# Moving one batch's normalisation ahead of another batch's scatter, from GpSimd to VectorE, and the next batch's projections to other units

## The chip, the core and the metric

The kernel runs on one core of one Trainium2 chip. The metric is device time in microseconds (us) of that core. Engines are named as in the profile: PE is TensorE, DVE is VectorE, ACT is ScalarE, POOL is GpSimd, SP is the engine that issues most DMAs. Each engine runs its own instruction stream in order and waits for the others on semaphores.

## The reference

The input is x of 8 batches x 512 tokens x 256 features, float32. Three sub-layers follow each other, each with a residual:

```
x = x + 0.5 * ffn(layernorm(x))
x = x + attn(layernorm(x))
x = x + 0.5 * ffn(layernorm(x))
```

`ffn` is a routed mixture of experts: a sigmoid picks one of 4 groups, the group's 2 experts (256 -> 512 -> 256, silu(gate) * up) are weighted by normalised sigmoid scores:

```
macro_scores = sigmoid(xf @ macro_w)            # 4 groups; the best one is taken
micro_scores = sigmoid(einsum('td,gde->tge', xf, micro_w))
out = einsum('te,tef,efd->td', w, silu(gate) * up, down_w)
```

`attn` has 16 heads of 16 features and works on windows of 128 tokens at a stride of 64, so 7 windows per batch:

```
scores = einsum('bhnqd,bhnkd->bhnqk', qw, kw) * scale + pos_bias
ow = einsum('bhnqk,bhnkd->bhnqd', softmax(scores), vw)
merged = zeros.at[:, :, flat].add(ow)           # overlapping windows are added,
merged = merged / counts                        # then divided by their count
return merged_as_rows @ Wo + bo
```

## The kernel before

The program has three stages. In the first, all 4096 tokens are normalised and routed; each token's row (its features, mean, reciprocal deviation, token number and two expert weights) is scattered to DRAM so that the tokens of a group lie together, and the first ffn goes over 35 tiles of 128 rows. The second stage is attention, and inside it, batch by batch, the routing for the second ffn. The third stage is the second ffn.

The change lies in the attention stage. A batch is 28 **units** (7 windows x 4 quarters of the heads); `batch(b, par, first_, last)` is written once for each engine. `two_by_two` (line 312) calls it for batch 0, then in a hardware loop of three turns for batches 1 and 2, 3 and 4, 5 and 6, then for batch 7. In a unit PE computes scores two units ahead (L1028, two units at a time), transposes four probability tiles (L846, `turn`) and multiplies with the values (L1055, `values`); DVE adds the bias and finds the row maximum two units ahead (L1491, `biased`), and copies the transposed probabilities out of PSUM (L1501, `copy_pt`); ACT takes the exponential (L806). After each window PE spreads the reciprocal sums (L1066, `factors`), DVE weighs the result (L1515, `weigh`) and POOL adds it into `ctxt` (L572, `accumulate`).

Between these, each unit has room for a piece of **side work**, and tables of unit numbers say which: `PE_SIDE`, `ACT_SIDE`, `DVE_SIDE` for a middle batch, `..._FIRST` for batch 0 and `..._LAST` for batch 7 (lines 281 to 300). DVE's table counts two units ahead and ACT's one behind: an entry at 16 in DVE's table runs in DVE's unit 14, one at 16 in ACT's in ACT's unit 17. While batch b runs, the side work is:

- for batch b+1: the norm (`bn_stats`, L1547, on DVE; the small arithmetic, L598 to L607, and the normalising itself, L612, on POOL), its transposes (`turn_prep`), their copies out of PSUM (`copy_prep`, L702, on ACT), and the projections to k and q (`k0a` to `q1b`, L983, copied out by ACT, L776 and L782) and to v (`v0` to `v3`, L998, copied out by DVE, L1481). Next batch's scores, which PE starts in unit 26, need all of k and q.
- for batch b-1: the output projection (`o0` to `o3`, L1011), the residual add on DVE (L1521), then the router: norm (`r_stat`, again with L612 on POOL), `turn_route`, logits (`l0` to `l3`), the exponential (L706), the best group (`best_groups`, L1256 to L1259, on DVE), `choose` (the first of equal groups, running counts, expert weights) and `find_place` on POOL, with PE's `rank` between them, and at last `scatter`: four indirect DMAs issued by POOL (L506), which write the batch's rows to their places.

POOL's order at a change of batch is what the change works on. At the end of batch b it runs `find_place` and `scatter` for batch b-1, and only then, at the head of batch b+1, `memset` of `ctxt` (L663) and `norm` for batch b+2, whose xa tiles PE's `turn_prep` waits for. In the middle batches `turn_prep` stands in unit 5 of PE. All DMAs of a batch but the scatter are issued by SP in order: the shifts of the values, the reload of `stage` with batch b-1's residual rows (L445), which must wait until the previous scatter has landed, and the load of `xb` for the norm (L428).

## Time and profile before

| | us |
|---|---|
| median of 3 runs | 1509.48 (1508.91 to 1517.62) |
| the profiled execution | 1505.25, span 1503.5 |
| attention stage, DVE's first copy of batch 0 to its first of batch 7 | 528.5 to 1054.9 |
| PE busy | 1254.1, 83% of the span |
| DVE busy | 842.9, 56% |
| ACT busy | 667.3, 44% |
| POOL busy | 372.3, 25% |

The shares are over the whole span; the attention stage is read by batch from the row of times in which each batch's 28 copies (L1501) start. The clock column of a window view is the mean TensorE clock granted in it: 1.00 is 2.4 GHz, 0.50 is 1.2 GHz. Idle time before an instruction is given in square brackets with what ended it.

### The profile page before, as it was taken

The page shows a single profiled execution, that of the slowest core. Times are in us where ns is not written, and L with a number is a line of the kernel's source. Part 1 is how long each engine was busy: PE and PEld are TensorE (multiplying, and loading weights), DVE is VectorE, ACT ScalarE, POOL GpSimd, SP SyncE. Part 2 cuts the span into 40 slices and gives each one's busy share as a digit, 9 for nine tenths or more (in the row PEclk, how much of TensorE's full clock was granted, in tenths as well). Part 3 has the DMA queues.
Part 4 walks back from the last instruction along what each step waited for, and adds up shares of the span by engine and source line. Part 5 has one row for each costly group of instructions (what it writes and reads, how often), then busy time and mean ns, then how long its engine had stood idle before and what let it go on. Part 6 is the DMA issues. An engine that isn't in the chain of part 4 may idle for free. (4 is left out here: it accounts for less than half of the span.)

```text
span 1503.5 us, 33781 instructions
## 1 busy us (share of the span) xinstructions
PE 1254.1 (83%) x8771; PEld 813.0 (54%) x8772; DVE 842.9 (56%) x3419; ACT 667.3 (44%) x2395; POOL 372.3 (25%) x624
## 2 busy tenths in 40 slices
PE   4422599999999499989899888989963899999997
PEld 4422366666666255555556555555542466666665
DVE  5689544444444277776667666757853344444443
ACT  1105322222323278776767676858750222223222
POOL 3322111111111322353434343443343011111111
PEclk9999999999999799998999899989975899999999
DMA  9600452000000310110010102020106121000000
GB/s 302 224 22 25 155 182 58 23 14 14 14 14 15 98 36 9 43 51 15 25 44 23 43 10 57 2 65 2 51 26 252 47 63 53 14 14 14 14 14 18
DMA packets 51758, 81.36 MB, mean 54 GB/s; under 512 B 7424, under 2 KB 35328, under 8 KB 51648
## 3 DMA queue, kind: packets, MB, share of 16 engines
q1 hardware_dynamic: 44832, 61.29, 12.8%
q0 software_dynamic: 6816, 18.81, 3.5%
q8 instruction: 45, 0.74, 0.2%
q14 instruction: 65, 0.53, 0.1%
HBM read 45.81 MB, written 27.97 MB: 49 GB/s over the span
## 5 line engine op out<-in xcount | busy, mean ns | idle before, releaser
L895 PE MATMUL bank<-w_all,xt 128*128 x1680 | 389.5, 382 | 11.7 <-DVE xt L1343 3.5
L806 ACT ACTIVATE w_all<-w_all 128x128 f32<-128x128 f32 x896 | 346.7, 392 | 95.1 <-DVE w_all L1491 93.4
L895 PEld LDWEIGHTS bank<-w_all,xt 128*128 128x128 f16 x1680 | 164.9, 98 | 195.7 <-issue 35.6
L1491 DVE CUSTOM_DVE_ANT_0 w_all<-bank,w_all 128x128 f32<-128x128 f32 x896 | 197.6, 285 | 77.6 <-ACT w_all L806 40.8
L1331 DVE SCALAR_TENSOR_TENSOR hb<-bank,ew,sl 128x512 f32<-128x512 f32 x140 | 105.1, 751 | 206.4 <-ACT sl L717 206.4
L913 PE MATMUL bank<-w_all,ht 128*128 x1680 | 206.2, 273 | 1.2 <-DVE yt L1356 1.2
L717 ACT ACTIVATE sl<-bank,back 128x512 f32<-128x512 f32 x140 | 95.8, 685 | 237.8 <-PE bank L895 224.9
L913 PEld LDWEIGHTS bank<-w_all,ht 128*128 128x128 f16 x1680 | 164.1, 98 | 19.4 <-issue 1.7
L806 ACT ACTIVATION_READ_ACCUMULATOR w_all<-w_all 128x1 f32 x896 | 171.3, 191 | 0.0
L846 PE MATMUL bank<-ident,w_all 128*128 128x128 f32 x896 | 154.0, 298 | 17.5 <-ACT w_all L806 11.1
L1501 DVE COPY w_all<-bank 128x512 f32<-128x512 f32 x224 | 152.0, 682 | 11.5 <-PE bank L1055 9.5
L846 PEld LDWEIGHTS bank<-ident,w_all 128*128 128x128 f32 x896 | 104.6, 149 | 88.8 <-issue 52.5
L721 ACT ACTIVATE xt<-bank 128x256 f16<-128x256 f32 x70 | 26.8, 383 | 245.6 <-PE bank L846 245.6
L846 PE MATMUL bank<-ident,xa 128*128 128x128 f32 x192 | 37.8, 361 | 103.7 <-DVE xa L1207 83.7
L1343 DVE SCALAR_TENSOR_TENSOR xt<-bank,xt 128x256 f16<-128x256 f32 x70 | 29.7, 425 | 159.4 <-ACT xt L721 159.4
L520 POOL DMA_INDIRECT mid<-yt,yidx x35 | 33.6, 959 | 301.3 <-DVE yt L1356 301.3
L520 POOL DMA_INDIRECT out<-yt,yidx x35 | 33.6, 959 | 299.6 <-DVE yt L1356 288.9
L572 POOL TENSOR_TENSOR ctxt<-ctxt,ct 128x256 f32<-128x256 f32 x56 | 40.6, 726 | 232.2 <-DVE ct L1515 232.2
L1349 DVE TENSOR_TENSOR ht<-bank,ht 128x512 f16<-128x512 f32 x140 | 95.2, 680 | 0.6 <-ACT ht L726 0.6
L846 PEld LDWEIGHTS bank<-ident,xa 128*128 128x128 f32 x192 | 30.1, 187 | 107.8 <-DVE xa L1207 51.8
L846 PE MATMUL bank<-ident,hb 128*128 128x128 f32 x560 | 84.1, 273 | 0.0
L726 ACT CAST ht<-bank 128x512 f16<-128x512 f32 x140 | 81.5, 582 | 2.1 <-PE bank L846 2.1
(214 smaller groups left out, 1708.3 us busy)
## 6 DMA issues: line engine op xcount, KB each, us to landing
big<-sorted_rows SPq DMA_DIRECT2D x70, 130.5 KB
saved<-w_all SPq DMA_DIRECT2D x16, 512.0 KB, 2.8
w_all<-saved SPq DMA_DIRECT2D x4, 2048.0 KB, 14.7
w_all<-mid SPq DMA_DIRECT2D x9, 512.0 KB, 4.0
big<-in_L_attn_hidden_states SPq DMA_DIRECT2D x8, 512.0 KB, 4.1
w_all<-in_L_ffn_gate_w SPq DMA_DIRECT2D x8, 512.0 KB
w_all<-in_L_ffn_up_w SPq DMA_DIRECT2D x8, 512.0 KB
w_all<-in_L_ffn_down_w SPq DMA_DIRECT2D x8, 512.0 KB
```

Of the source, the lines that this page charges most:

```text
L520: pool.indirect_dma_start(dst, bass.IndirectOffsetOnAxis(ap=yidx[:, 0:1], axis=0), yt[:], None).then_inc(y_scattered, 16)
L572: pool.tensor_tensor(win, win, ct[:, (par + n) % 2], ALU.add).then_inc(acc_done, 1)
L717: nc.scalar.activation(sl[:, e], bank[2 * e][:], ACT.Silu, scale=back[:, 0:1]).then_inc(silu_done, 1)
L726: nc.scalar.copy(ht[:, e, 0], bank[4 + e][:]).then_inc(ht_high, 1)
L806: a = nc.scalar.activation(prob[:, u % NB, h], sbias[:, u % NB, h], ACT.Exp, bias=nmax[:, u % NB, h:h + 1], scale=-1.0, accum_out=rsum[:, ...
L846: return nc.tensor.transpose(dst, src, ident[:])
L895: mm = nc.tensor.matmul(bank[2 * e + w][:], xt[:, hx, c, :], flat(gu16[:, bass.ds(g * E + e, 1), w, hw, c, :]), start=(i == 0), stop=(i == ...
L913: mm = nc.tensor.matmul(bank[6][:, 0:D], ht[:, e, hh, f * P:(f + 1) * P], flat(d16[:, bass.ds(g * E + e, 1), hw, f, :]), start=(e == 0 and ...
L1331: nc.vector.scalar_tensor_tensor(out=hb[:, e], in0=bank[2 * e + 1][:], scalar=ew[:, e:e + 1], in1=sl[:, e], op0=ALU.mult, op1=ALU.mult).th ...
L1349: nc.vector.tensor_tensor(ht[:, e, 1], bank[4 + e][:], ht[:, e, 0], ALU.subtract).then_inc(ht_ready, 1)
L1491: i = nc.vector.tensor_tensor_reduce(out=sbias[:, u % NB, h], in0=bank[u % 2][:, h * W:(h + 1) * W], in1=nbias[:, head_at(u % NQ, h)], sca ...
L1501: nc.vector.tensor_copy(pt_s[:, u % 2], bank[2 + u % 2][:]).then_inc(pt_ready, 1)
```

## The change

The normalising of both norms (L612 on POOL) becomes DVE's, four instructions a norm, split over units (`norm0` to `norm3`, `r_norm0` to `r_norm3`); POOL keeps the small arithmetic. The norm of batch b+2 is found at the end of batch b, in POOL's window 3 (`n == 3`) ahead of `choose` and `scatter`, and normalised in DVE's units 25 to 27; before, it came after the scatter. `turn_prep` moves from PE's unit 5 to unit 3, the k projections from 7, 8, 13, 14 to 4 to 7, q from 15, 16, 24, 25 to 13 to 16, v from 27, 1, 2, 3 to 24, 25 and the next batch's 0 and 1. The choice of the first of equal groups moves from four POOL instructions (`rest`) to three DVE instructions (`first`, one unit after `best`). SP loads `xb` before it waits for the scatter. Semaphores are split so that each of these has its own. PSUM banks 6 and 7 change roles for v and the output projection.

```diff
-        PE_SIDE = {1: ("v1",), 2: ("v2",), 3: ("v3",), 5: ("turn_prep",), 7: ("k0a",), 8: ("k0b",), 9: ("o0",),
-                   10: ("o1",), 11: ("o2",), 12: ("o3",), 13: ("k1a",), 14: ("k1b",), 15: ("q0a",), 16: ("q0b",),
-                   18: ("turn_route",), 20: ("l0",), 21: ("l1",), 22: ("l2",), 23: ("l3",), 24: ("q1a",), 25: ("q1b",),
-                   27: ("v0", "rank")}
+        PE_SIDE = {0: ("v2",), 1: ("v3",), 3: ("turn_prep",), 4: ("k0a",), 5: ("k0b",), 6: ("k1a",), 7: ("k1b",),
+                   9: ("o0",), 10: ("o1",), 11: ("o2",), 12: ("o3",), 13: ("q0a",), 14: ("q0b",), 15: ("q1a",), 16: ("q1b",),
+                   18: ("turn_route",), 20: ("l0",), 21: ("l1",), 22: ("l2",), 23: ("l3",), 24: ("v0",), 25: ("v1",),
+                   27: ("rank",)}
-        ACT_SIDE = {5: ("copy_prep",), 8: ("copy_k0",), 14: ("copy_k1",), 16: ("copy_q0",), 18: ("copy_route",),
-                    23: ("logits",), 25: ("copy_q1",)}
+        ACT_SIDE = {3: ("copy_prep",), 5: ("copy_k0",), 7: ("copy_k1",), 15: ("copy_q0",), 17: ("copy_q1",),
+                    19: ("copy_route",), 23: ("logits",)}
-        DVE_SIDE = {2: ("copy_v1",), 4: ("copy_v2", "copy_v3"), 10: ("add0",), 11: ("r_stat0", "add1"), 12: ("add2",),
-                    13: ("r_stat1", "add3"), 14: ("r_stat2", "r_stat3"), 20: ("stat0",), 22: ("stat1",), 24: ("best",),
-                    25: ("stat2",), 26: ("stat3",), 28: ("copy_v0",),
-                    29: ("place",)}
+        DVE_SIDE = {2: ("copy_v2", "copy_v3"), 10: ("add0",), 11: ("add1", "r_stat0"), 12: ("add2",),
+                    13: ("add3", "r_stat1"), 14: ("r_stat2", "r_stat3"), 16: ("r_norm0", "r_norm1"),
+                    17: ("r_norm2", "r_norm3"), 18: ("stat0",), 19: ("stat1",), 21: ("stat2",), 22: ("stat3",),
+                    24: ("best",), 25: ("first",), 26: ("copy_v0", "copy_v1"), 27: ("norm0", "norm1"), 28: ("norm2",),
+                    29: ("place", "norm3")}
...
@@ SP, batch
+                if not last and not first_:
+                    sp.wait_ge(xa_prep, (b + 1) * TB)
+                    load_batch(b + 2)
                 if not first_:
                     sp.wait_ge(scattered, (b - 1) * (16 * TB) + 16 * TB * B)
                     sp.dma_start(stage[:, :, 0:D], rows_of(b - 1)).then_inc(res_loaded, 16)
-                if not last:
-                    sp.wait_ge(xa_ready, (prep_use(b + 1) + 1) * TB)
+                if first_:
+                    sp.wait_ge(xa_prep, (b + 1) * TB)
                     load_batch(b + 2)
@@ POOL, norm
-                pool.tensor_tensor(rstd, var, mhalf[:], ALU.pow).then_inc(rstd_ready, 1)
-                pool.wait_ge(rstd_ready, k + 1)
-                pool.wait_ge(xnt_psum, k * DC + OPEN)
-                pool.sem_inc(pool_open, 1)
-                for t in range(TB):
-                    pool.tensor_scalar(xa[:, t, :], src[:, t, 0:D], mean[:, t:t + 1], rstd[:, t:t + 1],
-                                       ALU.subtract, ALU.mult).then_inc(xa_ready, 1)
+                pool.tensor_tensor(rstd, var, mhalf[:], ALU.pow).then_inc(found, 1)
@@ POOL, choose
-                step(pool.tensor_scalar(rest[:, :, 1:G], eq[:, :, 0:G - 1], -1.0, 1.0, ALU.mult, ALU.add))
-                step(pool.tensor_tensor(rest[:, :, 2], rest[:, :, 2], rest[:, :, 1], ALU.mult))
-                step(pool.tensor_tensor(rest[:, :, 3], rest[:, :, 3], rest[:, :, 2], ALU.mult))
-                pool.tensor_tensor(oh[:], eq[:], rest[:], ALU.mult)
@@ POOL, batch
                 pool.memset(ctxt[par][:], 0.0).then_inc(ctx_zero, 1)
-                if not last:
-                    norm(prep_use(b + 1), stat_ready, b + 1, stats, xb, mean_b[:], ln_t[:, 4, :])
+                if first_:
+                    norm(0, stat_ready, 1, stats, mean_b[:], ln_t[:, 4, :], prep_rstd)
...
-                        norm(route_use(b - 1), r_stat_ready, b, stats_r, stage, stage[:, :, C_MEAN], stage[:, :, C_RSTD])
+                        norm(b * 2, r_stat_ready, b, stats_r, stage[:, :, C_MEAN], stage[:, :, C_RSTD], route_rstd)
+                    if n == 3 and not last:
+                        norm(b * 2 + 1, stat_ready, b + 2, stats, mean_b[:], ln_t[:, 4, :], prep_rstd)
@@ DVE, normalise and best_groups
-            def normalise(k, src, mean, rstd):
-                dve.wait_ge(rstd_ready, k + 1)
+            def normalise(k, src, mean, rstd, found, n, said, tiles_=range(TB)):
+                dve.wait_ge(found, n)
...
+                nc.vector.tensor_tensor(eqw[:], eq[:], bc(gweight[:], 1, [P, TB, G]), ALU.mult).then_inc(eqw_ready, 1)
+                dve.wait_ge(eqw_ready, r - B + 1)
+                dve.sem_inc(unit_open, 1)
+                step(nc.vector.tensor_reduce(first[:], eqw[:], AX.X, ALU.max))
+                nc.vector.tensor_tensor(oh[:], eqw[:], bc(first[:], 2, [P, TB, G]), ALU.is_equal).then_inc(first_ready, 1)
```

POOL, from the scatter at the end of a middle batch to the head of the next, before. `stats` and `ln_t` are the norm's, `ctxt` is the accumulator.

```order
L506 DMA sorted_rows<-stage,pos 17024x261 x4
L660 ISA
L663 MEMSET ctxt 128x1024
L594 REGISTER_ALU
L598 TENSOR_TENSOR ln_t<-stats 128x4
...
L607 TENSOR_TENSOR ln_t<-ln_t,mhalf 128x4
L608 REGISTER_ALU
L609 ISA
L612 TENSOR_SCALAR xa<-w_all,mean_b,ln_t 128x256 x4
L569 REGISTER_ALU
L572 TENSOR_TENSOR ctxt<-ctxt,ct 128x2x128
```

The same place with the change:

```order
L513 DMA sorted_rows<-stage,pos 17024x261 x4
L657 ISA
L660 MEMSET ctxt 128x1024
L576 REGISTER_ALU
L579 TENSOR_TENSOR ctxt<-ctxt,ct 128x2x128
L583 REGISTER_ALU
L584 TENSOR_TENSOR stage<-stage,w_all 128x4x256
```

The whole norm has left the place behind the scatter: the accumulation and the bias of the residual follow the memset directly.

DVE, the last two units of a middle batch with the change (L1503 is `copy_pt`, L1517 `weigh`, L1510 the reciprocal, L1201 the normalising):

```order
L1503 COPY w_all<-bank 128x512
L1513 REGISTER_ALU
L1517 TENSOR_TENSOR ct<-bank,w_all 128x256
L1201 TENSOR_SCALAR xa<-w_all,mean_b,ln_t 128x256
L1503 COPY w_all<-bank 128x512
L1510 RECIPROCAL w_all<-w_all 128x16
L1570 TENSOR_TENSOR place<-bank,gcap 128x16
L1201 TENSOR_SCALAR xa<-w_all,mean_b,ln_t 128x256
```

Two of the four normalising instructions stand here, two one unit earlier; before, this place had the copy of v0 and no normalising.

PE, around the start of the next batch's scores (unit 26), before (L983 is the second half of `q1`, L1028 the scores):

```order
L846 MATMUL bank<-ident,w_all 128x128 x4
L1055 MATMUL bank<-w_all,va 32x128 x4
L983 MATMUL bank<-xnt,w_all 128x512
L1019 ISA
L1023 REGISTER_ALU
L1028 MATMUL bank<-big,w_all 128x256 x4
```

With the change (L995 is the second v projection, L1025 the scores):

```order
L845 MATMUL bank<-ident,w_all 128x128 x4
L1052 MATMUL bank<-w_all,va 32x128 x4
L995 MATMUL bank<-w_all,xnt 128x256 x2
L1016 ISA
L1020 REGISTER_ALU
L1025 MATMUL bank<-big,w_all 128x256 x4
```

The scores now follow a v projection, and the last q projection stands ten units earlier.

## Rows read from the trace of the kernel before

**Rows 1.** Windows, batches 1 to 6; columns: us, busy (count) by engine, clock, DMA
```profile
593.40:662.55 69.15, 65.49 (x561) 41.45 (x562) 52.26 (x288) 54.84 (x251) 26.33 (x52) 1.00 0.10 29
662.55:743.33 80.78, 71.00 (x563) 44.70 (x564) 52.32 (x290) 55.16 (x251) 34.32 (x65) 0.92 0.12 33
743.33:819.25 75.92, 69.59 (x559) 43.31 (x558) 52.17 (x288) 55.26 (x251) 30.89 (x62) 0.93 0.11 31
819.25:899.94 80.69, 70.89 (x562) 44.66 (x563) 52.31 (x288) 55.16 (x251) 34.13 (x65) 0.92 0.11 32
899.94:976.06 76.12, 69.81 (x560) 43.59 (x559) 52.19 (x290) 55.21 (x251) 31.09 (x62) 0.93 0.11 32
976.06:1054.90 78.84, 70.66 (x561) 44.55 (x562) 52.40 (x290) 55.24 (x252) 32.59 (x63) 0.91 0.11 32
```

**Rows 2.** Waits of PE from 528.5 to 1116 us: total, times, longest
```profile
PE bank L846 <- POOL xa L612: 19.8, 6, 5.1
PE bank L846 <- ACT w_all L806: 11.1, 28, 1.2
PE bank L1028 <- DVE w_all L1491: 5.6, 12, 1.5
PE bank L846 <- DVE w_all L1501: 5.6, 7, 1.5
PE bank L1028 <- ACT w_all L782: 4.7, 3, 1.6
PE bank L1028 <- ACT qt L782: 4.7, 3, 1.6
PE bank L1028 <- issue: 4.1, 3, 1.6
```

**Rows 3.** Timeline of PE in batch 2: start, duration, instruction, idle before
```profile
677.25 1.97 PE L846 MATMUL bank<-ident,xa 128*128 128x128 f32 x8 [5.09 <-POOL xa L612]
679.15 2.08 PE L1028 MATMUL bank<-big,w_all 32*128 32x256 f32 x8
681.16 1.11 PE L846 MATMUL bank<-ident,w_all 128*128 128x128 f32 x4
...
690.97 1.13 PE L1028 MATMUL bank<-big,w_all 32*128 32x256 f32 x8
692.26 0.66 PE L846 MATMUL bank<-ident,w_all 128*128 128x128 f32 x4 [0.15 <-ACT w_all L806]
```

**Rows 4.** Timeline of POOL at the start of batch 2
```profile
662.78 1.11 POOL L506 DMA_INDIRECT sorted_rows<-stage,pos  x1 [0.85 <-POOL pos L654]
...
667.70 0.97 POOL L663 MEMSET ctxt<- 128x1024 f32 x1
...
672.34 4.85 POOL L612 TENSOR_SCALAR xa<-w_all,mean_b,ln_t 128x256 f32<-128x256 f32 x4 [0.32 <-POOL ln_t L607]
```

**Rows 5.** Windows of lowered clock: two of ten, and the sum of all ten
```profile
674.50:684.75 10.25, 7.50 (x41) 4.92 (x42) 2.38 (x17) 5.47 (x25) 5.52 (x5) 0.50 0.29 101
...
732.50:735.95 3.45, 3.45 (x28) 1.84 (x24) 2.38 (x17) 2.27 (x13) 1.65 (x4) 0.51 0.01 2
...
sum 61.75, PE 54.27 PEld 33.97 DVE 23.80 ACT 41.54 POOL 27.73; mean PE 5.43 PEld 3.40 DVE 2.38 ACT 4.15 POOL 2.77
```

**Rows 6.** Timeline of PE in unit 26 of batch 2
```profile
731.69 1.31 PE L1028 MATMUL bank<-big,qt 32*128 32x256 f32 x8 [1.56 <-ACT qt L782]
```

**Rows 7.** Groups of instructions, 500 to 1120 us: busy us, mean ns, idle before
```profile
L612 POOL TENSOR_SCALAR xa<-w_all,mean_b,ln_t 128x256 f32<-128x256 f32 x28 | 34.0, 1223 | 2.1 <-POOL ln_t L607 2.1
...
L1259 DVE TENSOR_TENSOR eq<-sg,best 128x16 f32<-128x16 f32 x7 | 1.2, 175 | 0.2
```

**Rows 8.** Page, part 6, DMA issues: count, size, us from issue to landing
```profile
w_all<-mid SPq DMA_DIRECT2D x9, 512.0 KB, 4.0
```

**Rows 9.** Timeline of PE behind the last batch, its output projection
```profile
1131.77 5.44 PE L1011 MATMUL bank<-w_all,ctxt 128*128 128x256 f32 x16 [12.81 <-POOL ctxt L572]
```

**Rows 10.** Timeline of DVE behind the last batch, its normalising
```profile
1141.31 1.38 DVE L1207 TENSOR_SCALAR xa<-stage 128x256 f32<-128x256 f32 x4 [1.16 <-POOL stage L497]
```

More of the change, by code:

```diff
@@ L124, in macaron_kernel @@
         stats_r = sb("stats_r", [P, TB, 6])
-        rest = sb("rest", [P, TB, G])
         minus = sb("minus", [P, TB])
@@ L302, in steps @@
+        DVE_LAST = {2: ("copy_v2", "copy_v3"), 10: ("add0",), 11: ("add1", "r_stat0"), 12: ("add2",),
+                    13: ("add3", "r_stat1"), 14: ("r_stat2", "r_stat3"), 16: ("r_norm0", "r_norm1"),
+                    17: ("r_norm2", "r_norm3"), 24: ("best",), 25: ("first",), 28: ("place",)}
         def steps(u, first_, last, side, side_first, side_last):
@@ L475, in _ @@
         def _(pool):
-            for v, c in ((ident, 0.0), (tri, 1.0), (ones, 1.0), (mhalf, -0.5), (pads, 0.0), (seen, 0.0), (rest, 1.0), (minus, -1.0)):
+            for v, c in ((ident, 0.0), (tri, 1.0), (ones, 1.0), (mhalf, -0.5), (pads, 0.0), (seen, 0.0), (minus, -1.0)):
                 pool.memset(v[:], c).then_inc(const_made, 1)
@@ L536, in _ @@
                     power(r + 1, ln_t[:, 5, :], rows_in(r + 1, tiles)[:, :, C_RSTD])
-                scatter(r, r, rows_in(r, tiles), r)
+                scatter(r, (rstd_ready, r + 1), rows_in(r, tiles), r)
             scatter_pads(0)
@@ L590, in __call__, with norm @@
                     pool.sem_inc(pool_open, 1)
[L592 removed]
+            def norm(i, said, n, st, mean, rstd, found):
                 pool.wait_ge(said, n)
                 pool.sem_inc(pool_open, 1)
[L596 removed]
+                step = Chain(p_norm, i * PNORM_STEPS)
                 s, d, v, dd, _, var = (ln_t[:, i, :] for i in range(6))
@@ L678, in batch @@
                     find_place(b + (B - 1), B, step)
-                    scatter(b + (B - 1), route_use(b - 1), stage, B)
+                    scatter(b + (B - 1), (route_rstd, b), stage, B)
             two_by_two(pool, batch)
@@ L683, in _ @@
             accumulate(B - 1, 1, NWIN - 1)
-            power(route_use(B - 1), ln_t[:, 5, :], stage[:, :, C_RSTD], B + 1)
-            scatter(2 * B - 1, route_use(B - 1), stage, B)
+            power(B + 1, ln_t[:, 5, :], stage[:, :, C_RSTD])
+            scatter(2 * B - 1, (rstd_ready, B + 2), stage, B)
             scatter_pads(1)
@@ L992, in project_v @@
                     pe.wait_ge(q_ready, b * DC + DC)
-                if t == 1:
-                    pe.wait_ge(v_ready, b * TB + 1)
                 if t == 2:
-                    pe.wait_ge(pos_ready, b + (B - 1))
+                    pe.wait_ge(v_ready, b * TB + 2)
                 for c in range(DC):
@@ L1116, in batch @@
                             if t < 2:
-                                ready = (v_ready, b * TB + TB)
-                                if t == 1 and not last:
-                                    ready = (k_ready, b * DC + (DC + 1))
+                                ready = (k_ready, b * DC + (DC + t + 1))
+                                if last:
+                                    ready = ((pos_ready, b + (B - 1)), (v_ready, b * TB + TB))[t]
                             project_out(b - 1, 1 - par, t, ready)
@@ L1556, in batch @@
                                 i.then_inc(r_stat_ready, 1)
-                        if s in ("copy_v1", "copy_v2", "copy_v3"):
+                        if s in ("norm0", "norm1", "norm2", "norm3"):
+                            i = b + (1 if first_ and u + 2 < 9 else 2)
+                            normalise(prep_use(i), xb, mean_b[:], ln_t[:, 4, :], prep_rstd, i, xa_prep, (int(s[-1]),))
+                        if s in ("r_norm0", "r_norm1", "r_norm2", "r_norm3"):
+                            normalise(route_use(b - 1), stage, stage[:, :, C_MEAN], stage[:, :, C_RSTD], route_rstd, b,
+                                      xa_route, (int(s[-1]),))
+                        if s in ("copy_v2", "copy_v3"):
                             copy_v(b, par, int(s[-1]))
@@ L1564, in batch @@
                         if s == "best":
-                            best_groups(b + (B - 1))
-                        if s == "copy_v0":
-                            copy_v(b + 1, 1 - par, 0)
+                            parts = best_groups(b + (B - 1))
+                        if s in ("best", "first"):
+                            next(parts)
+                        if s in ("copy_v0", "copy_v1"):
+                            copy_v(b + 1, 1 - par, int(s[-1]))
                         if s in ("add0", "add1", "add2", "add3"):
```

111 lines of the change are left out of this document (56 added, 55 removed).

## The prediction, written before the change was run

> **What bounds the kernel now.** First I read the attention stage by batch [rows 1]. In each middle batch PE is busy 65.5 to 71.0 us; the next are ACT with 55 and DVE with 52, and POOL has 26 to 34. So PE is the engine to follow there, and POOL's small share says that it can only hurt by being late. The reader should compare the batches among themselves: batches 1 to 6 do the same PE work (559 to 563 matmuls), and yet batch 1 takes 69.15 us and batches 2 to 6 take 75.92 to 80.78. Batch 1 is the only one that no scatter of a former batch precedes, and the only one whose clock column reads 1.00; the others read 0.91 to 0.93.
>
> Then the waits of PE in the stage [rows 2]. The longest in total is POOL's `xa` (L612), 19.8 us in 6 waits; the copies of the q projection (L782) give 9.4 us in 6; the rest, ACT's exponentials, DVE's bias and copies, is 22.3 us in many small pieces, and `issue`, mostly the return of the hardware loop, is 4.1.
>
> The timelines show the mechanism. In batch 2 POOL starts the first indirect DMA at 662.78, is through with the memset at 668.7, does the small arithmetic of the norm, and starts the four L612 instructions only at 672.34; they take 4.85 us [rows 4]. PE waits 5.09 us for them and resumes at 677.25 [rows 3]. By then the granted clock is half (1.2 GHz): the windows of lowered clock begin at 674.5, while PE stood idle, and PE has 7.50 us of work in that one [rows 5]. The same instructions take 2.08 and 1.11 us there and 1.13 and 0.66 us at 2.4 GHz [rows 3]. A second, shorter window of lowered clock, 3.4 us, lies in batches 2 to 6 just after PE's unit-26 wait of 1.56 us for the copy of q1 [rows 5, 6]; batch 1 has such a wait too and keeps its clock, so that a fall follows in five cases of six. The ten windows hold 54.27 us of PE work [rows 5].
>
> **The change, part by part.**
>
> (a) *The norm leaves the place behind the scatter.* PE's waits on L612 go: 19.8 us [rows 2]. The cover is long: xa is now ready at the end of the batch before, and `turn_prep` is asked for in unit 3 of the next; the other things it waits for (the v copies of DVE's unit 0, and `pos` from POOL, which stands 1 us before the first scatter DMA [rows 4]) are some 7 us earlier than PE gets there.
>
> (b) *q1 is projected in units 15 and 16, not 24 and 25.* Its copy is then ready ten units ahead of the scores: 4.7 + 4.7 = 9.4 us [rows 2].
>
> (c) *The clock.* By the pairs of rows 3, (2.08 + 1.11) / (1.13 + 0.66) = 1.78, so 1 - 1/1.78 = 44% of PE's time in the windows is loss: 0.44 x 54.27 = 23.9 us [rows 3, 5]. All ten windows follow one of the waits of (a) or (b), so I let all go.
>
> (a) to (c) give 53.1 us. A check from the other side: batch 1 without its 1.56 us is 67.6. Batches 2 to 6 sum to 392.4 [rows 1], 54.4 above 5 x 67.6. Two loop returns fall in them; at 1.6 us of `issue` and 1.5 of a late DVE copy each [rows 2] that is 6.2, which stays. 48.2 remain, with batch 1's 1.6 and about 1 in batches 0 and 7 nearly 51. Between the two I take 52.
>
> (d) *Added on DVE.* 56 normalising instructions (7 batches, two norms of four) at 1.38 / 4 = 0.345 us [rows 10]: 19.3 us; POOL spends 1.22 on each [rows 7]. The `first` part is three small DVE instructions and one handshake, about 3 x 0.175 + 0.2 = 0.7 us [rows 7], 7 times: 5. Together 24 us, from 0 (all in DVE's idle time, 69.15 - 52.26 = 17 us a batch [rows 1]) to 24 (all in the path). PE now waits 11.2 us in total for DVE's ordinary work [rows 2] of over 400 us, so it is nearly hidden; but with PE's batch shorter, DVE rises from 76% busy to (52.3 + 3.4) / 68 = 82%, and ACT from 79% to 81%. I take 7, nearer the lower end. Queued behind a normalising instruction are DVE's bias and `copy_pt`, which ACT and PE wait for; each pair of tiles pushes them back by 0.7 us, less than a unit's work of PE.
>
> The Trainium skill's page "VectorE: DVE Perf Modes" (section "The perf-mode tier table (the rule you actually need)") gives an fp32 tensor_scalar from SBUF to SBUF twice the plain rate. The trace does not agree for 256 elements: 0.345 us each [rows 10] is little less than one element per cycle at the 0.96 GHz the page names. By the page's fixed 58 cycles and the doubled rate each would take an estimated 0.19 us, and (d) would begin at 11 + 5 us, not 24.
>
> (e) *DVE waits for POOL's norm.* `r_norm0` stands in DVE's unit 14, two units after the last `r_stat`. POOL's small arithmetic from memset to L612 takes 672.34 - 668.67 = 3.7 us [rows 4], two units about 5. For the prep norm there are five units. I take 0; the upper bound is in the rivals.
>
> (f) *ACT's copies move into busier units.* The copy of q1 now stands in ACT's unit 18, and `turn_route` waits for it. No row shows this; the nearest is the present wait for the same copy, 1.56 us [rows 6], so 0 to 1.5 us in each of six batches. The exponential of unit 18 is done before it, and PE has a transpose and the values between; I take 0. The k projections follow their transposes by one unit instead of two, with the same bounds, also 0.
>
> (g) *The scatter's own path and SP's queue.* POOL's four `rest` instructions go, three on DVE come a unit later: no change for `rank`. SP issues the `xb` load ahead of the reload of `stage`: a load lands in 4.0 us [rows 8] and `stage` is needed for the adds in DVE's unit 8, some 15 us after the scatter. Cost 0; without that cover, up to 4 us a batch. POOL's `accumulate` and bias come 9 us earlier.
>
> (h) *Ends.* The first and third stages, 12.81 us of waiting for POOL behind the last batch [rows 9] included, do the same. v1 moves from batch 7 to the prologue's side: 0 in all.
>
> Sum: 52 - 7 = 45 us. The profiled execution took 1505.25 us (span 1503.5), so 1460; the median shown is 4.2 above it, so **1464 us**.
>
> **Rivals.**
>
> 1. *Most of (d) and (f) shows.* DVE and ACT become co-bounds, PE waits for the late copies. Gain 52 - 24 - 5 = 23: 1486. For it: three engines above 80%, coupled two units deep. Against it: batch 1, which runs at 69 us with all side work but the normalising. Half of this gives 1475.
>
> 2. *The clock still falls.* Small waits remain, two at the loop's return, and the five short windows come back elsewhere: 17.3 us of PE work x 0.44 = 7.6 [rows 5], 1472.
>
> 3. *DVE and POOL lock each other out.* If a normalising group must wait for POOL's instruction in progress, of about 0.97 us [rows 4], 14 groups cost 13.6: 1478. Against it: DVE's present 0.345 us shows plain rate. The Trainium skill's page "SBUF — State Buffer" (section "🔬 SBUF: two separate sides") names this lock for VectorE's two-port modes; by that rule and the tier table together this rival would be the case, by the trace's rate it would not.
>
> 4. *Slower: the in-order wait of (e) decides.* If POOL reaches the small arithmetic late (it stands behind `accumulate`, which waits for DVE's `weigh`), DVE stands still at `r_norm0` or `norm0`, nothing behind it runs, PE starves and the clock falls too. A 5.09 us wait costs about 5.1 + 0.44 x 7.5 = 8.4 us [rows 3, 5]. To end slower by 1% the 52 gained and 15 more must be lost, 67 / 8.4 = 8 such waits of 14 places: above 1525. It would start where POOL is more than 1.3 us (5 - 3.7) behind, and needs 5 us beyond. POOL has 40 us a batch idle, so I doubt it.
>
> 5. *The change misses its aim:* xa comes late for another reason (`pos_ready`, `v_ready`), (a) and its clock windows stay; only (b) and its windows go, 9.4 + 7.6 - 7 = 10: 1499.
>
> **How the numbers follow.** Chances: forecast 0.56 (1455 to 1470); rival 1 0.18; 2 0.12; 3 0.04; 4 0.03; 5 0.03; better than 1455, because DVE's other waits go as well, 0.04. What a measurement of this kernel can tell from no change is about 1%, so faster means under 1494.4. Low end: 52 + 5 of the late copies with nothing lost to (d), 1509.5 - 57 = 1452. High end: rival 1's full price, 1486. Faster 0.93, same 0.04, slower 0.03.
>
> **What would show it.** PE's batches 1 to 6 at 67 to 70 us each, clock column near 1.00, no wait of PE on `xa` above 1 us in units 3 to 5, none on L782's copies, POOL's normalising gone and DVE's at 0.35 to 0.41 us each, DVE's busy time per batch near 56. Wrong if new waits of PE on DVE's bias or copies sum to over 20 us, if DVE waits for `rstd` on POOL, or if windows of 1.2 GHz persist in most batches; if batches still differ by the scatter before them, the place of the norm was not the cause.

## The result, and the profile after

The changed kernel takes **1469.32 us** (median of 4 runs, 1466.65 to 1473.65), the kernel before 1509.20 beside it; the ratio is 0.9731, 95% interval 0.9684 to 0.9777. The forecast was 1464, with 1452 to 1486 as its range. The profiled execution took 1468.96 us (span 1467.2, mean clock 0.964), against 1505.25 (1503.5) before: 36.3 us less.

Windows of the changed kernel's batches 1 to 7, the answer to [rows 1] (columns: from:to, length, busy us of each engine with its count, granted clock, DMA share, GB/s):

```profile
593.26:661.12 67.86, 64.80 (x555) 40.87 (x557) 55.14 (x301) 54.85 (x251) 17.55 (x46) 1.00 0.11 29
661.12:732.64 71.52, 66.12 (x553) 41.47 (x554) 55.27 (x301) 54.98 (x251) 24.66 (x53) 0.96 0.13 38
732.64:804.56 71.92, 69.02 (x572) 43.59 (x575) 55.24 (x301) 55.18 (x251) 20.52 (x49) 0.97 0.12 33
804.56:876.43 71.87, 66.12 (x553) 41.48 (x554) 55.27 (x299) 54.98 (x251) 24.90 (x54) 0.96 0.13 37
876.43:948.18 71.75, 68.84 (x572) 43.62 (x575) 55.23 (x301) 55.07 (x251) 20.27 (x49) 0.97 0.12 33
948.18:1016.68 68.50, 65.59 (x565) 41.47 (x568) 55.17 (x301) 54.96 (x251) 22.61 (x51) 1.00 0.13 37
1016.68:1079.21 62.53, 54.11 (x501) 35.92 (x500) 48.45 (x257) 45.97 (x221) 18.36 (x37) 0.94 0.09 27
```

Batches 1 to 6 take 423.4 us where they took 461.5, so all of the gain is in them; what lies around them gives back 1.8 (batch 7 alone is 2.0 longer). A batch's length is PE's busy time plus its idle time, and both fell. Busy: 417.4 to 400.5, for the same work, which is the clock: the windows of lowered clock in these batches held 54.27 us of PE's work and now hold 16.76 (below), and 44% of the difference is 16.5. Idle: 44.06 to 22.94. Batches 1 and 6 keep the full clock and take 67.9 and 68.5 us; batches 2 to 5, around the loop's two inner returns, take 71.5 to 71.9.

PE's waits in the changed kernel from 520 to 1085 us (columns: us in total, times, longest), the answer to [rows 2]:

```profile
PE bank L1025 <- DVE w_all L1493: 15.0, 27, 2.0
PE bank L845 <- ACT w_all L805: 14.4, 19, 1.5
PE bank L1025 <- issue: 5.3, 2, 2.8
PE bank L845 <- DVE w_all L1503: 3.6, 4, 2.2
```

There is no wait on `xa` any more and none of the scores on q's copy (now L781). But two others have grown. [rows 2] begins at 528.5 us; over the stretch of the kernel before that answers to this one (520 to 1121 us) the first of them reads

```profile
PE bank L1028 <- DVE w_all L1491: 7.6, 13, 2.0
```

and is 15.0 now, and the transposes' wait for ACT's exponentials has gone from 11.1 to 14.4. In batches 1 to 6 alone, PE waited 19.4 us for `xa`, 9.4 for q's copy, 3.7 for DVE's copies of the probabilities, 5.5 for the exponentials, 2.1 for the biased rows and 3.2 in `issue`; now it is 0, 0, 0, 9.8, 7.4 and 5.3. PE's timeline of batch 2 at the turn of the next batch's rows, the answer to [rows 3]:

```profile
665.96 1.04 PE L845 MATMUL bank<-ident,xa 128*128 128x128 f32 x8
666.93 1.13 PE L1025 MATMUL bank<-big,w_all 32*128 32x256 f32 x8
667.99 0.66 PE L845 MATMUL bank<-ident,w_all 128*128 128x128 f32 x4
```

No idle time stands in front, and eight transposes take 1.04 us where they took 1.97. The windows of lowered clock that are left, three in batches 1 to 6 and the fourth in batch 7 (columns: from:to, length, PE busy, clock, DMA share, GB/s), the answer to [rows 5]:

```profile
726.95:733.78 6.83, 5.19 (x24) 0.50 0.13 44
754.26:757.67 3.41, 3.41 (x18) 0.50 0.00 0
870.31:880.55 10.24, 8.16 (x39) 0.50 0.16 55
1054.63:1058.04 3.41, 3.41 (x22) 0.50 0.00 0
sum 23.89, PE 20.17; mean PE 5.04
```

The ten of [rows 5] all lay in batches 1 to 6, where three are left: 16.76 us of PE's work at 1.2 GHz in place of 54.27. The one in batch 7 is new. The first and the third begin in the pauses at the loop's return, which were 1.6 us; the first is now as below, the other 2.85:

```profile
728.59 2.07 PE L1025 MATMUL bank<-big,qt 32*128 32x256 f32 x8 [2.49 <-issue]
```

The normalising itself (one instruction's form in the changed kernel; duration min/median/max in ns) takes as long as the same form took on DVE in the kernel before (406 ns in the median, behind the last batch); the 0.345 us of [rows 10] is the mean distance between the starts of four in a row, and a little shorter:

```profile
L1201 DVE TENSOR_SCALAR xa<-w_all,mean_b,ln_t x36: 393/402/952, 506.5 to 1014.7; 128x256 f32<-128x256 f32 x36
L1201 DVE TENSOR_SCALAR xa<-stage x32: 313/408/819, 630.4 to 1105.8; 128x256 f32<-128x256 f32 x32
```

### The profile page after: what moved, and what is told of

Its sections match the earlier page's. It is cut to its first block and busy times, and to the rows that moved or that the text cites. A ratio compares the mean times of both kernels' runs of the same rounds, so it can differ in the third digit from the quotient of the medians.

```text
span 1467.2 us, 33794 instructions
## 1 busy us (share of the span) xinstructions
PE 1237.6 (84%) x8771; PEld 804.0 (55%) x8772; DVE 866.5 (59%) x3500; ACT 666.9 (45%) x2395; POOL 305.3 (21%) x548
## 5 line engine op out<-in xcount | busy, mean ns | idle before, releaser
L912 PEld LDWEIGHTS bank<-w_all,ht 128*128 128x128 f16 x1680 | 164.2, 98 | 19.4 <-issue 1.7
L845 PE MATMUL bank<-ident,w_all 128*128 128x128 f32 x896 | 146.1, 286 | 18.4 <-ACT w_all L805 14.4
L1503 DVE COPY w_all<-bank 128x512 f32<-128x512 f32 x224 | 152.3, 682 | 3.1 <-PE bank L1052 2.9
L845 PEld LDWEIGHTS bank<-ident,w_all 128*128 128x128 f32 x896 | 100.5, 143 | 85.3 <-issue 50.1
L579 POOL TENSOR_TENSOR ctxt<-ctxt,ct 128x256 f32<-128x256 f32 x56 | 42.4, 757 | 227.4 <-DVE ct L1517 227.1
L1025 PE MATMUL bank<-big,qt 32*128 32x256 f32 x448 | 65.4, 410 | 12.9 <-DVE w_all L1493 7.5
```

The costliest lines, as they stand in the source:

```text
L845: return nc.tensor.transpose(dst, src, ident[:])
L912: mm = nc.tensor.matmul(bank[6][:, 0:D], ht[:, e, hh, f * P:(f + 1) * P], flat(d16[:, bass.ds(g * E + e, 1), hw, f, :]), start=(e == 0 and ...
L1025: mm = nc.tensor.matmul(bank[q % 2][:, c * 2 * W:(c + 1) * 2 * W].rearrange("p (e k) -> p e k", e=2), qt[par][rows, c, win], km[par][rows, ...
L1503: nc.vector.tensor_copy(pt_s[:, u % 2], bank[2 + u % 2][:]).then_inc(pt_ready, 1)
```

## The experiments

The ratio is that to runs of the kernel before made beside each (their medians were 1507.4 to 1509.2 us), from all runs; the differences in us below are between medians. The other columns come from one profiled execution each, in us: the length of batches 1 to 6, PE's idle time in them, the lowered clock in them, and the length of batch 7. In the two warm kernels the dummies count as busy. A profile is one draw: the kernel with q1 early alone was profiled in a run of 1498 with a median of 1509, the written-out kernel before in one of 1524 with a median of 1515, the one with k1's copy late in one of 1473 with a median of 1466.

| kernel | median | ratio (95%) | b1-6 | idle | low clock | b7 |
|---|---|---|---|---|---|---|
| before | 1509.2 | 1 | 461.5 | 44.1 | 61.4 | 60.6 |
| order alone, written out | 1498.0 | 0.993 (0.990-0.996) | 451.2 | 38.4 | 47.8 | 61.0 |
| q1 early alone | 1509.1 | 1.0015 (0.998-1.005) | 456.0 | 38.1 | 61.4 | 60.6 |
| changed, q1 late | 1510.3 | 1.0003 (0.998-1.0025) | 455.5 | 39.2 | 54.6 | 70.9 |
| changed, norm behind scatter | 1487.3 | 0.984 (0.982-0.986) | 439.0 | 26.7 | 41.0 | 68.3 |
| changed, POOL normalises | 1479.0 | 0.980 (0.974-0.987) | 426.3 | 25.3 | 13.7 | 72.8 |
| changed | 1469.3 | 0.973 (0.968-0.978) | 423.4 | 22.9 | 20.5 | 62.5 |
| changed, k1's copy late | 1465.7 | 0.971 (0.970-0.972) | 418.0 | 18.3 | 17.1 | 67.1 |
| before, written out | 1515.0 | 1.003 (1.000-1.007) | 467.9 | 46.6 | 75.1 | 67.4 |
| changed, written out | 1474.5 | 0.975 (0.970-0.981) | 417.4 | 21.6 | 3.4 | 71.8 |
| before, warm 8 and 3 | 1510.9 | 1.0001 (0.997-1.003) | 457.8 | 24.6 | 23.9 | 60.5 |
| before, warm 5 and 1 | 1505.1 | 0.9965 (0.993-1.000) | 451.4 | 26.2 | 34.1 | 59.4 |
| changed, scatter twice | 1528.9 | 1.012 (1.006-1.0175) | 461.6 | 42.9 | 54.6 | 78.2 |
| changed, no memset | 1476.6 | 0.979 (0.9735-0.984) | 425.6 | 25.4 | 13.7 | 67.2 |

### The order alone

```diff
 # before, POOL, end of a batch; the loop over batches written out
     if not first_:
         find_place(b + (B - 1), B, step)
+    if b + 2 < B:
+        norm(prep_use(b + 2), stat_ready, b + 2, stats, xb, ...)
+    if not first_:
         scatter(b + (B - 1), route_use(b - 1), stage, B)
```

> The kernel before with its batch loop written out and one move: POOL finds and applies the norm of the next batch before the scatter instead of behind it; POOL still normalises, projections stay at their units. Theory A (the place of the norm is the cause): PE's waits on xa of 2 to 5 us in batches 2 to 6 (19.4 us) and the long windows of 1.2 GHz behind them (37 us of PE work, 16 us lost) go: 35 us less than the written-out kernel before, about 1469. Rival B (POOL's slow normalising, 4 x 1.22 us, is the cause): POOL is merely early by 5 us of scatter, waits of 1 to 2 us stay, 10 us less or fewer, 1490 or more.

Measured: 1498.0 us, 17 less than the written-out kernel before and 11 less than the kernel before. Theory A expected 35 and rival B 10 or fewer, so neither holds. PE's waits (520 to 1095 us) hold next to nothing on `xa`, but:

```profile
PE bank L849 <- ACT w_all L809: 27.0, 34, 3.7
PE bank L1031 <- DVE w_all L1494: 8.4, 13, 2.0
...
PE bank L1031 <- ACT w_all L785: 4.5, 3, 1.5
PE bank L1031 <- ACT qt L785: 4.4, 3, 1.5
```

The order does take the wait on `xa` away, as term (a) says. Most of it comes back as waits for ACT (11.1 to 27.0). In batch 2, which begins at 664.1, POOL now issues its indirect DMAs from 672.2 to 677.1; VectorE has pauses of 1.49 and 1.70 us and ScalarE one of 1.53 beside them, and PE then waits 3.70 us for an exponential (see the scatter, below). And the late q1 stays.

### q1 early alone

```diff
-13: ("k1a",), 14: ("k1b",), 15: ("q0a",), 16: ("q0b",), ... 24: ("q1a",), 25: ("q1b",),
+13: ("k1a", "k1b"), 14: ("q0a",), 15: ("q0b",), 16: ("q1a",), 17: ("q1b",), ...
```

> The kernel before, with the second query group projected early alone: k1 in unit 13, q0 in 14 and 15, q1 in 16 and 17, its copy behind unit 17; in the first batch q1 in units 17 and 18. POOL still normalises, behind the scatter. Theory A (the prediction's terms are separate): the waits of 1.56 us at unit 26 go, 9.4 us, with the five short windows of the lower clock behind them, 7.6 us, less about 3 for fuller units 13 to 17: 1495 us. Theory B (with q1 late the changed kernel ran like the kernel before, so the late q1 is what holds everything): 1475 us or less. Theory C (the two parts only pay together): 1503 us or more.

Measured: 1.0015, theory C. The waits on q's copy (9.4 us) are gone from the profile and the idle time in batches 1 to 6 fell by 6.0 us, but the time at lowered clock stayed at 61.4. One window alone is as long as two of before (columns as above):

```profile
732.30:752.80 20.50, 20.09 (x98) 0.50 0.14 42
```

PE's gaps ahead of it are 0.59, 1.03 and 0.54 us. So a long wait in front is not needed for a fall, and taking one away need not keep the clock up.

### q1 late in the changed kernel

```diff
-15: ("q1a",), 16: ("q1b",), ... 24: ("v0",), 25: ("v1",), 27: ("rank",)}
+... 24: ("q1a",), 25: ("q1b",), 27: ("v0", "v1", "rank")}
```

> The changed kernel, with the second query group's projections back behind units 24 and 25 and the value projections behind unit 27, as before the change; the norm stays ahead of the scatter and stays on VectorE. It prices the term of the prediction on unit 26. Theory A: TensorE waits 1.56 us for the copy in unit 26 again, in seven batches 10.9 us, and the clock falls again behind that wait (3.4 us of the slower clock in the batches, 0.44 of it lost, 1.5 us each), 10 to 18 us more than the changed kernel, forecast 1483 us. Theory B (the wait only lay beside another, and the values' copies of VectorE in the busy units cost as much): within 4 us of 1469.

On VectorE the copies of v0 and v1 move with them, into one entry with `place` and the last normalising instruction. Measured: 1.0003. The whole gain is gone, 41 us where theory A expected 10 to 18 and theory B under 4. PE's timeline in unit 26 of batch 2:

```profile
734.30 1.72 PE L1025 MATMUL bank<-big,qt 32*128 32x256 f32 x8 [2.17 <-ACT qt L781]
735.96 1.11 PE L845 MATMUL bank<-ident,w_all 128*128 128x128 f32 x4
```

The wait is 2.17 us, against 1.56 in [rows 6], and the window of lowered clock behind it is 6.8 us (734.7 to 741.5) against 3.4. Batches 1 to 6 give back 32.1 us: 16.3 more idle, and 15.8 more busy at the lower clock. Batches 0 and 7 are 3.7 and 8.4 us longer in this profile, with windows of their own. The expectation priced one fall of 3.4 us in each batch; there are 10 windows with 54.6 us in batches 1 to 6, six of them 6.8 us long behind the q1 wait of each batch. Of the idle time that came back 13.0 us are the waits on q's copy. The run is not q1's alone: the scores' wait for DVE rose from 15.0 to 19.1 us, and what the moved v copies did to it wasn't measured apart.

### The norm behind the scatter again, VectorE still normalising

```diff
-PE_SIDE = {..., 3: ("turn_prep",), 4: ("k0a",), 5: ("k0b",), 6: ("k1a",), 7: ("k1b",),
+PE_SIDE = {..., 5: ("turn_prep",), 6: ("k0a",), 7: ("k0b", "k1a"), 8: ("k1b",),
+DVE_SIDE = {..., 5: ("norm0", "norm1", "norm2", "norm3"),   # no longer in 27 to 29
```

> The changed kernel, with the next batch's statistics finished by POOL behind the scatter again, as before the change; VectorE still normalises, behind unit 5, and the turn of the normalised rows moves to unit 5, the key projections to units 6 to 8. It prices the order alone, where the run with the order alone on the kernel before priced it from the other side. Theory A: POOL's chain ends at about 11 us behind the batch's start and VectorE's four steps of 0.4 us behind it, so TensorE waits 1.6 to 5 us in each of six batches, and the clock falls behind it: 15 to 35 us more than the changed kernel, forecast 1490 us. Theory B (with VectorE normalising, rstd comes early enough by itself, the order is worth nothing): within 5 us of 1469.

The turn of the normalised rows stands two units later here, and the k projections closer together. Measured: 0.984, 18 us more than the changed kernel; theory A, at its low end. PE in batch 2:

```profile
672.14 1.97 PE L840 MATMUL bank<-ident,xa 128*128 128x128 f32 x8 [1.02 <-DVE xa L1196]
674.04 2.08 PE L1020 MATMUL bank<-big,w_all 32*128 32x256 f32 x8
```

The wait is 1.02 us, a fifth of that before; with 2.21 us in batch 4 and one more it makes 3.8 in all. The clock was down when it came: it fell at 669.6, behind another pause of 1.22 us, for biased rows of VectorE, which had itself stood 1.59 us beside the scatter. Batches 2, 4 and 6 take 76.6, 77.1 and 74.0 us against 71.5, 71.9 and 68.5.

### POOL normalises, the order as changed

```diff
     pool.tensor_tensor(rstd, var, mhalf[:], ALU.pow).then_inc(found, 1)
+    pool.wait_ge(found, have)
+    for t in range(TB):
+        pool.tensor_scalar(xa[:, t, :], src[:, t, 0:D], mean[:, t:t + 1], rstd[:, t:t + 1],
+                           ALU.subtract, ALU.mult).then_inc(told, 1)
```

> The changed kernel with the normalising (both norms) given back to POOL, all else as changed, the prep norm ahead of the scatter. Theory A (the order pays, the engine hardly): PE finds xa ready in units 3, waits at most 1 us in unit 18, DVE is 2.8 us a batch less busy; within 6 us of 1469. Rival B (the engine pays): waits on xa of 2 us or more come back in unit 18 and late scatters hold the next batch, 1480 or more.

Measured: 0.980, 10 us more than the changed kernel, between theory A (up to 6) and rival B (1480 us or more); the two intervals overlap at their ends. In batches 1 to 6 it is only 2.9 us slower (426.3 against 423.4). The rest is batch 7 with 72.8 against 62.5 us, which holds 28 us of lowered clock. PE's waits, 520 to 1095 us:

```profile
PE bank L852 <- ACT w_all L812: 15.9, 20, 1.2
PE bank L1032 <- DVE w_all L1500: 13.6, 25, 2.0
```

They are about as large as in the changed kernel though VectorE normalises nothing. So those new waits are not the price of the moved normalising. The other part of term (d), the choice of the first group, is still on VectorE here.

### The loop written out

```diff
-with eng.Fori(1, B // 2) as i:
+for i in range(1, B // 2):
     batch(i * 2 - 1, 1, False, False)
     batch(i * 2, 0, False, False)
```

Done on the kernel before:

> The kernel before with the hardware loop over batches 1 to 6 written out, nothing else. Theory A (returning to the loop's head costs PE and DVE 1.5 us each, twice): about 5 us less, 1504; PE's waits named issue (4.1 us) go. Rival B: the pauses at the change of batch belong to the dependence between batches, no change.

and on the changed one:

> The changed kernel with the loop over batches written out. Theory A: batches 2 to 5 (71.5 to 71.9 us) come down to batch 6's 68.5, 13 us less: 1456; the windows of 1.2 GHz behind the returns go too. Rival B (code loading costs the same written out, or the pauses are dependences): within 3 us of 1469.

Measured: 1.003 and 0.975, so no gain from either where theory A expected 5 and 13 us; the kernel before does what its rival B said, the changed one is 5 us slower and fits neither theory. Before, PE's waits named issue went from 4.1 to 0.8 us, but the waits on `xa` are 26.6 us, not 19.8 (in a profile 10 us above the median): the pause at the return had probably covered part of POOL's lateness. After, batches 2 to 6 run at 69.3 to 71.1 us with a single short fall, as theory A said, but batches 0 and 7 are 3.8 and 9.3 us longer, with falls of their own.

### Keeping PE busy in its wait

```diff
 # before, PE, ahead of the turn of the normalised rows
     pe.wait_ge(v_ready, b * TB + TB)
+    if not first_:
+        for _ in range(3 if par else 8):        # second run: 1 if par else 5
+            nc.tensor.matmul(bank[7][:], ident[:], xnt[:, 0, :], start=True, stop=True)
     turn_batch(prep_use(b + 1))
```

> The kernel before, with dummy matmuls in front of TensorE's wait for the normalised next batch (8 in batches that end a loop body, 3 in the others), so that TensorE is busy in that wait and the wait itself stays as long as it was. It separates what the wait costs from what the lower clock behind it costs. Theory A (the clock falls because TensorE idles in that wait): the windows of the lower clock at 674 to 685 us and their repeats at 831 and 988 go, each 10.2 us long and worth 0.44 of it, 13.5 us in three, and the short ones behind the single waits at unit 26 stay; forecast 1498 us, against 1509 of the kernel before. Theory B (the falls have nothing to do with the gap in front of them): the windows stay at their places and the dummies cost up to 1 us each batch, 1509 to 1515 us.

> The kernel before, with 5 dummy matmuls in batches that end a loop body and 1 in the others in front of TensorE's wait for the normalised batch; with 8 and 3 TensorE was still busy with them 1.8 us after the rows were ready. They take 0.89 us each, 4.5 us of a wait of 5.1. It prices the clock's fall behind that wait alone. Theory A: three long falls go, each worth the 3.1 us by which the same instructions ran shorter behind the wait in the run with 8 dummies, 9 us less, batch 1 0.9 longer and two falls behind the 2.04 us waits partly gone: 1497 us. Theory B (a fall that is kept off in one place comes in another, as in the run with 8): 1505 to 1511 us.

Measured: 1.0001 and 0.9965. With 8 and 3 dummies the windows behind the waits go, as theory A said, but the dummies run 1.8 us past the rows' arrival, a window of 6.8 us comes at 658 in batch 1 (5.1 us longer, its three dummies included), and two of the short windows behind unit 26, at 736 and 965, are 6.8 us in place of 3.4. The total lies in theory B's range, though its windows didn't stay. With 5 dummies, PE in batch 2:

```profile
673.25 4.56 PE L1094 MATMUL bank<-xnt,ident 128*128 128x512 f32 x10
678.40 1.09 PE L846 MATMUL bank<-ident,xa 128*128 128x128 f32 x8 [0.60 <-POOL xa L612]
679.43 1.13 PE L1028 MATMUL bank<-big,w_all 32*128 32x256 f32 x8
```

The rows come at the same point as before, but PE goes on at the full rate (1.09 and 1.13 us against 1.97 and 2.08 in [rows 3]). Batches 2, 4 and 6 are 4.5, 3.1 and 3.3 us shorter: that is what a long fall behind the wait cost, and 0.44 x 7.5 = 3.3 had said so. The short fall at the end of batch 2 began 3 us later and ran on into batch 3, 13.7 us in one where there had been 3.4 and 6.8, and batch 3 gained nothing. The 10 runs spread from 1495 to 1512. Their median lies at the near end of theory B's 1505 to 1511, and four of the runs near theory A's 1497; the price is shown in the batches, and the total does not decide.

### k1's copy one unit later

In the changed kernel PE stands 1.06 us in unit 9 of batches 1 to 6. PE's and ACT's rows in batch 2:

```profile
680.55 0.66 PE L845 MATMUL bank<-ident,w_all 128*128 128x128 f32 x4 [1.06 <-ACT w_all L805]
```

```profile
677.52 1.45 ACT L775 ACTIVATE big<-bank,w_all 128x512 f32<-128x512 f32 x2 [1.06 <-PE bank L982]
```

ACT stands 1.06 us for a projection that PE has only just issued, with the exponentials queued behind. In the kernel before k1's copy followed its projection as closely, in unit 15, and ACT stood 0.60 us.

```diff
-ACT_SIDE = {3: ("copy_prep",), 5: ("copy_k0",), 7: ("copy_k1",), ...
+ACT_SIDE = {3: ("copy_prep",), 5: ("copy_k0",), 8: ("copy_k1",), ...
```

> The changed kernel, with one number moved: ACT's copy of the second key group goes from behind unit 7 to behind unit 8. In the changed kernel TensorE stands 1.06 us before the turn of unit 9 in every batch from 1 to 6, because ACT's exponential of unit 9 is queued behind that copy, and the copy waits for a projection that TensorE itself only issues in unit 7. Theory A (what the changed kernel still waits for is ACT's and VectorE's order in single units): unit 9 loses its wait in seven batches, 7 x 1.06 = 7.4 us less, forecast 1462 us. Theory B (ACT and VectorE are full there in any case, and the wait only moves to the next unit): no change, 1468 to 1470 us, the gap shows before the turn of unit 10.

Measured: 1465.68 us, the lowest median of all, 3.6 under the changed kernel; theory A expected 7.4. The wait is gone in each of batches 1 to 6, and batches 1 to 6 take 5.4 us less (418.0). Five of 7 runs took 1464.1 to 1465.9 us and two 1473.3 and 1477.9. The interval overlaps the changed kernel's, so the total does not settle that it is the better one; the batches say so.

### The scatter twice, and no memset

```diff
     pool.indirect_dma_start(sorted_rows, ..., rows[:, t, :], None).then_inc(scattered, 16)
+    if twice:      # in the attention stage
+        pool.indirect_dma_start(other_rows, ..., rows[:, t, :], None).then_inc(scattered, 16)
```

> The changed kernel, with each indirect DMA of the attention stage's scatter issued twice, the second into another tensor of the same size, which nobody reads: POOL issues 8 in place of 4 a batch. In the profiles VectorE's copy and ScalarE's work stand still for 1.5 to 2 us while POOL issues these DMAs and its memset. Theory A (POOL's issue of indirect DMAs holds VectorE): the stall doubles in seven batches, 1.5 to 2 us each, 10 to 14 us more than 1469. Theory B (the stall belongs to the memset, or is none of POOL's): within 4 us of 1469, since POOL is idle 40 us a batch.

```diff
-pool.memset(ctxt[par][:], 0.0).then_inc(ctx_zero, 1)
+if first_:
+    pool.memset(ctxt[1][:], 0.0)
+    pool.memset(ctxt[0][:], 0.0).then_inc(ctx_zero, 1)
+else:
+    pool.sem_inc(ctx_zero, 1)
```

The second kernel leaves the clearing of the accumulator out, so the batches' contexts add up in it.

> The changed kernel, with POOL's memset of the context tile (128x1024, 0.97 us) left out from batch 1 on, so that contexts of batches add up in it; everything else as it was. Theory A (VectorE stands while POOL's memset writes, a lock of the two engines, the third rival of the prediction): the copies behind it come 1 to 2 us earlier in six batches, 6 to 12 us less, 1460 us. Theory B (the memset is free): within 4 us of 1469.

Measured: 1.012 and 0.979. The doubled scatter costs 60 us, over four times what theory A gave it. In batches 1 to 6 it is 38.2: 20.0 more idle, and 18.2 more busy at the lower clock. POOL, VectorE, ScalarE and PE in batch 2 of that kernel:

```profile
666.75 1.11 POOL L514 DMA_INDIRECT sorted_rows<-stage,pos  x1 [0.85 <-POOL pos L655]
...
675.77 0.96 POOL L517 DMA_INDIRECT other_rows<-stage,pos  x1 [0.30 <-issue]
676.73 0.97 POOL L664 MEMSET ctxt<- 128x1024 f32 x1
```

```profile
678.62 0.69 DVE L1507 COPY w_all<-bank 128x512 f32<-128x512 f32 x1 [7.83 <-remote]
```

```profile
678.82 1.07 ACT L705 COPY xnt<-bank 128x512 f32<-128x512 f32 x2 [7.61 <-remote]
```

```profile
672.70 0.27 PE L849 MATMUL bank<-ident,xa 128*128 128x128 f32 x1 [0.73 <-issue]
674.15 0.27 PE L849 MATMUL bank<-ident,xa 128*128 128x128 f32 x1 [1.19 <-issue]
674.91 0.45 PE L1029 MATMUL bank<-big,w_all 32*128 32x256 f32 x1 [0.49 <-issue]
677.04 0.58 PE L1029 MATMUL bank<-big,w_all 32*128 32x256 f32 x1 [1.67 <-issue]
```

All three compute engines stand, PE in the middle of a group and with nothing that the profile shows to wait for. VectorE and ScalarE go on 1.9 and 2.1 us behind the last of the eight DMAs, PE 0.3. From 670.7 to 678.9 us, the time of that pause, the DMA queues moved

```profile
q1 hardware_dynamic: 720, 0.82, 37.9%
q0 software_dynamic: 288, 0.80, 28.2%
```

(packets, MB, share of 16 engines) and nothing for the two queues that bring instructions, so the engines were not seen waiting for code. Whether it is the issuing or the transfers themselves that they stand for is not separated. Batches 2 to 6 are 3.5 to 9.3 us longer than in the changed kernel, batch 7 15.7, and batch 1, ahead of the first scatter, not at all. Without the memset the same pause as before stands around the end of the four DMAs (666.17) in VectorE's timeline:

```profile
667.55 0.69 DVE L1507 COPY w_all<-bank 128x512 f32<-128x512 f32 x1 [2.08 <-remote]
```

So the memset is not its cause, and theory A of that run fell. Theory B missed as well, by 7 us: batches 1 to 6 are 2.2 us longer and batch 7 4.7, with 17.6 us of lowered clock.

## Why the prediction was right, and where it was short

The forecast took 52 - 7 = 45 us off the profiled execution and 36.3 came: inside the range, and 5 us off the median. The mechanism was right in kind, two late waits and the clock behind them, and the clock was taken too high. By its steps:

(a) and (b), **the two waits**: gone to the last microsecond. That they could be added up from a table was wrong. Alone, the order gives 11 us (17 against the written-out kernel) and the early q1 none; the changed kernel without its early q1 is at 1510 and without its order at 1487. Together with the change's other moves, and POOL still normalising, they give 30. In these runs each wait that stayed kept a stretch in which the clock fell, or, as with the order alone, another engine became late at the next place.

(d) and (f), **new waits**: 7 us were taken. PE's idle time in batches 1 to 6 fell by 21.1 us, against 29.2 - 7 = 22.2 forecast for the stage, so the size was right. The cause given was not. Of term (d), the 19 us of normalising on VectorE cost nothing that can be found, since with POOL normalising the waits are about the same; its other 5 us were not tested. What cost was a copy of the kind of (f), which was put at 0: k1's, which waits for its own projection in unit 7 and made 1.06 us in each of six batches, 6.4 in all. (f) had priced q1's copy and the distance of the k projections from their transposes, not this one; the experiment that moved it got 5.4 us back. The growth of the waits on biased rows in the same batches, from 2.1 to 7.4 us, has no cause shown.

(c), **the clock**: this is the step that failed in size. "All ten windows follow one of the waits of (a) or (b), so I let all go" was true of the order in time. Of the cause it was true in part: the dummies show it for the long windows, but with the waits of (b) alone taken away the lowered clock stayed at 61.4 us. Of 23.9 us, 16.9 came (PE's busy time 417.4 to 400.5). The 7.0 missing are close to the price of the second rival, in which the clock still falls (7.6), and to 44% of the 16.76 us left (7.4). Two of the windows now begin in the pause at the loop's return, and one behind the 1.06 us wait for k1's copy.

The sum closes: 7.0 less from the clock, 1.1 less idle time won and 1.8 given back around the batches are 9.9; the forecast had taken 52 for the 53.1 of (a) to (c), which leaves 8.8, and 45 - 8.8 is 36.2. The sign named for the batches, 67 to 70 us each, was met by two of six.

The rest: the loop's returns were allowed 6.2 us that stay. Batches 2 to 5 are 3.0 to 3.4 us longer than batch 6, 13 in all, and falls of the clock are part of that. Removing the returns wins 6.1 us in batches 1 to 6 and loses 13 in batches 0 and 7. No wait on POOL's `rstd` appears in batches 1 to 6, so (e) holds. (g), the scatter's own path at 0, holds as far as the batches show; but it left out that the other engines can stand beside POOL's DMAs, so that it matters what stands there.

The third rival, VectorE and POOL locking each other out, is seen on a small scale. 59 of the 68 normalising instructions took 313 to 442 ns, eight took 814 to 821 and one 952. Each of those nine began 0.14 to 0.22 us behind the start of an instruction of POOL, `accumulate` (L579) in eight cases and the memset in one, and ended 0.15 us behind its end; the 15 that began just ahead of an `accumulate` took 396 to 414. The written-out changed kernel shows the same. VectorE's and POOL's rows in batch 1:

```profile
630.37 1.14 DVE L1201 TENSOR_SCALAR xa<-stage 128x256 f32<-128x256 f32 x2
630.53 0.82 POOL L579 TENSOR_TENSOR ctxt<-ctxt,ct 128x256 f32<-128x256 f32 x1 [0.36 <-DVE ct L1517]
```

It is the second of the pair that took 0.81 us. The price is 0.4 us once a batch, not 0.97 at each of 14 groups. The first rival (both co-bound), the fourth (an in-order wait) and the fifth (`xa` late for another reason) did not come.

## What to carry to other kernels

Price a wait from the trace, but do not add up the clock behind several waits: in these runs a fall often moved to the next gap when its own was taken away. So remove all large waits of a stage together, and test each part both alone and taken out of the whole, because here a part worth nothing alone went with the whole gain when it was taken out. When side work moves to another unit, look first at the engine behind it in order (here ScalarE's copy that waited for PE's last issue), rather than at the busy shares.

## What the runs showed of the hardware that was not expected

The other engines stand still beside POOL's indirect DMAs. Four in a row (0.96 to 1.11 us each) go with a pause of VectorE of 2.05 us in the kernel before and 2.08 and 2.09 in two of the changed ones; in batches 2, 4 and 6 of the changed kernel itself there is none over 0.94, so it isn't so each time. Eight give 7.83, ScalarE 7.61, and PE pauses of 0.49 to 1.67 us inside a group. Which resource they share is open. The Trainium skill's page "SBUF — State Buffer" (section "🔬 SBUF: two separate sides") describes a port that VectorE and GpSimd share and lock, and says that PE and ScalarE never wait for one. Here ScalarE (7.61 us) and PE (up to 1.67) stood too, so that lock alone does not explain these rows. That taking the existing scatter out would win time wasn't tried.

One normalising instruction of VectorE in each batch took twice its time (0.82 for 0.41 us) when POOL's `accumulate` was under way as it began, which is how the lock of the third rival would look; that it is the lock is not shown.

Falls of the clock began in or just behind gaps of PE of 5.09, 2.04, 1.56 and 1.06 us, and in one kernel of 0.59, 1.03 and 0.54; other gaps of 1.56 and 1.06 us were followed by none. Executions of one kernel differ by it: the kernel with 5 dummies took 1495.3 to 1497.4 us in four runs at a mean clock of 0.959 to 0.963, and 1504.9 to 1511.9 in six at 0.948 to 0.953. A change of under 1% in this kernel is therefore read in the lengths of single batches sooner than in the median.
